# Moving the weight buffers of a fused decoder layer by 896 bytes, and reordering queues around its second batch

## The reference

```
h = rmsnorm(x) * norm_w
q, k, v = heads(h Wq), heads(h Wk), heads(h Wv)      # 8 heads of 64, q and k rotated (rope)
f, g, o = sigmoid(h Wbeta + b), sigmoid(h Wig + b), sigmoid(h Wog + b)
M_t = f_t * M_(t-1) + g_t/8 * k_t v_t^T ;  y_t = (q_t M_t) * o_t      # for each head
x = layernorm(x + y Wout + bout)
r_t = 0.9 r_(t-1) + ctx_t^2 ;  x = layernorm(x + x * r)
# 4096 tokens in 4 micro batches; 8 experts, each 128 tokens of every micro batch
x = layernorm(x + gelu(norm(x) W1_e + b1_e) W2_e + b2_e)      # 512 -> 2048 -> 512
```

## Time and profile before

| | |
|---|---|
| median of 3 runs | 1263.2 us (1260.92 to 1263.53) |
| the profiled execution | 1261.89 us |
| its span, first to last instruction | 1260.1 us |
| TensorE busy | 1240.9 us, 98% of the span |
| VectorE, GpSimd, ScalarE busy | 62%, 59%, 37% |
| DMA | 142 GB/s in the mean |
| granted TensorE clock | 1.00 throughout |

### The profile page before, as it was taken

One profiled execution on the slowest core, in us unless ns is written; L12 is line 12 of the kernel. 1 busy time (PEld: TensorE's weight loads), 2 busy tenths in 40 slices (PEclk: granted clock), 3 DMA queues, 4 the chain that ended last, 5 costly groups with the idle time before them and its releaser, 6 DMA issues.

```text
span 1260.1 us, 19325 instructions
## 1 busy us (share of the span) xinstructions
PE 1240.9 (98%) x6682; PEld 1010.0 (80%) x6682; DVE 782.8 (62%) x1297; ACT 460.9 (37%) x629; POOL 737.7 (59%) x519
## 2 busy tenths in 40 slices
PE   8999999999999999999999999999999999999998
PEld 7777888888888888778888888888888888888886
DVE  5898888888888888953544544634734535445424
ACT  5223333333333322544434443534435344343420
POOL 4876665656566665667457275284385384472651
PEclk9999999999999999999999999999999999999999
DMA  7778887877876786536316235245073073162310
GB/s 274 157 152 161 162 160 154 159 160 160 161 160 155 160 156 123 144 141 242 100 60 225 91 108 197 71 169 180 28 248 126 0 275 100 51 232 94 118 51 33
DMA packets 178107, 179.52 MB, mean 142 GB/s; under 512 B 44732, under 2 KB 121484, under 8 KB 178060
## 3 DMA queue, kind: packets, MB, share of 16 engines
q1 hardware_dynamic: 177548, 178.64, 53.0%
q10 hardware_dynamic: 512, 0.26, 0.1%
HBM read 137.55 MB, written 17.18 MB: 123 GB/s over the span
## 4 chain that ended last, share of the span: by engine, by line
PE 60%; DVE 1%; issue 0%; POOL 0%; ACT 0%; POOLq 0%; DVEq 0%; ACTq 0%
PE qk_ps L87 5%; PE qk_ps L89 5%; PE qk_ps L88 5%; PE v_ps L87 5%; PE v_ps L89 5%; PE v_ps L88 5%; PE gate_ps L87 5%; PE gate_ps L89 5%; PE gate_ps L88 5%; PE s_ps L87 3%; PE s_ps L89 3%; PE s_ps L88 3%; PE y_ps L87 3%; PE y_ps L89 2%; PE y_ps L88 2%
## 5 line engine op out<-in xcount | busy, mean ns | idle before, releaser
L1006 POOL TENSOR_TENSOR w_lo<-w_raw,w_hi 128x2048 fp32r<-128x2048 f32 x31 | 143.4, 4626 | 101.3 <-ACT w_hi L760 101.3
L1342 DVE CAST hid_hi<-gate_ps 128x512 fp32r<-128x512 f32 x62 | 42.8, 690 | 196.8 <-ACT gate_ps L800 184.5
L998 POOL TENSOR_TENSOR w_lo<-w_raw,w_hi 128x2048 fp32r<-128x2048 f32 x32 | 148.0, 4626 | 13.6 <-ACT w_hi L770 13.6
L1088 DVE TENSOR_TENSOR_SCAN decays<-f_all,diag 128x384 f32<-128x384 f32 x128 | 151.0, 1218 | 0.6
L87 PE MATMUL qk_ps<-xT_parts,wqkv_hi 128*128 128x256 f32 x512 | 148.3, 290 | 1.7 <-ACT c_both L688 0.8
L89 PE MATMUL qk_ps<-xT_parts,wqkv_lo 128*128 128x256 f32 x512 | 144.4, 282 | 0.0
L88 PE MATMUL qk_ps<-xT_parts,wqkv_hi 128*128 128x256 f32 x512 | 144.2, 282 | 0.0
L1342 DVE CAST hid_hi<-v_ps 128x512 fp32r<-128x512 f32 x62 | 42.8, 690 | 148.2 <-ACT v_ps L800 148.2
L800 ACT ACTIVATE v_ps<-v_ps,b_cols 128x512 f32<-128x512 f32 x64 | 42.4, 662 | 198.9 <-PE v_ps L89 198.9
L87 PEld LDWEIGHTS qk_ps<-xT_parts,wqkv_hi 128*128 128x128 f32 x512 | 96.4, 188 | 12.7 <-issue 7.9
L800 ACT ACTIVATE gate_ps<-gate_ps,b_cols 128x512 f32<-128x512 f32 x64 | 42.2, 659 | 175.9 <-PE gate_ps L89 175.6
(11 more groups left out here) (238 smaller groups left out, 3221.0 us busy)
## 6 DMA issues: line engine op xcount, KB each, us to landing
w_raw<-in_w SPq DMA_DIRECT2D x64, 1024.0 KB, 7.8
f_all<-f_dram SPq DMA_DIRECT2D x16, 1024.0 KB, 5.0
qkT<-rot SPq DMA_DIRECT2D x256, 64.0 KB, 2.0
xT_raw<-in_xT SPq DMA_DIRECT2D x16, 512.0 KB, 12.9
x_both<-in_x SPq DMA_DIRECT2D x16, 512.0 KB, 11.6
f_all<-f_dram SPq DMA_DIRECT2D x16, 512.0 KB, 6.1
c_both<-in_ctx_in SPq DMA_DIRECT2D x16, 512.0 KB, 13.5
x_both<-x_dram SPq DMA_DIRECT2D x8, 1024.0 KB, 5.0
```

The lines of the kernel that those rows point to most:

```text
L998: pool.tensor_tensor(w2_lo[s % 2][:], w2_raw[s % 2][:], w2_hi[s % 2][:].bitcast(F32), ALU.subtract)\
L1006: pool.tensor_tensor(w1_lo[s % 2][:], w1_raw[s % 2][:], w1_hi[s % 2][:].bitcast(F32), ALU.subtract)\
L1088: dve.tensor_tensor_scan(decays[:, n, :], f_all[:, n, :], diag[:], 0.0, ALU.mult, ALU.add).then_inc(decay_done, 1)
L1342: dve.tensor_copy(high, up_ps[c % 2][:]).then_inc(hid_hi_done, 1)
```

## The change

SBUF_FROM goes up by 896 bytes and wg_parts, which takes 896 bytes, moves from between wqkv_lo and wout_hi to behind res. So wqkv_hi and wqkv_lo (and all that the experts keep in them) move up by 896 bytes, wout_hi to res stay where they were, and the small buffers behind move up by 896.

In the first batches the orders change. TensorE: shares 6 and 7 of batch 1 come ahead of the first scores of batch 0, and share 8 and turn_gates(1) ahead of the second. VectorE: sum_gates(2) ahead of scans 6 and 7 of batch 1; in the last batch scan 6 behind token_low 1 and 2. ScalarE: the gates of batch 2 no longer wait until the scans of batch 1 are done (they had protected f_all); SP waits for that instead, ahead of the loads of f_all. SP: x of batch 3 is loaded behind the moves of batch 1, and the three constants of the experts behind the gates' loads. GpSimd: context_low(0) ahead of the third rotation of batch 1, residual(1) behind the fourth.

```diff
--- before.py
+++ after.py
@@ -45,7 +45,7 @@
 DW = P + L
 RMS_EPS, LN_EPS = 1e-6, 1e-5
 DECAY, THETA = 0.9, 10000.0
-SBUF_FROM = 16512
+SBUF_FROM = 17408
 
 
 class Step:
@@ -127,8 +127,6 @@
 
     wqkv_hi = sb("wqkv_hi", [P, KC, 3 * D], F32R)
     wqkv_lo = sb("wqkv_lo", [P, KC, 3 * D], F32R)
-    wg_parts = sb("wg_parts", [P, KC, LOW_ROW + NG], F32R)
-    wg_hi, wg_lo = wg_parts[:, :, 0:NG], wg_parts[:, :, LOW_ROW:]
     wout_hi = sb("wout_hi", [P, KC, D], F32R)
     wout_lo = sb("wout_lo", [P, KC, D], F32R)
     bout_all = sb("bout_all", [P, 1, D])
@@ -169,6 +167,8 @@
     ctx_parts = sb("ctx_parts", [P, 2 * NT, D], F32R)
     ctx_hi, ctx_lo = ctx_parts[:, 0:NT, :], ctx_parts[:, NT:2 * NT, :]
     res = sb("res", [P, NT, D])
+    wg_parts = sb("wg_parts", [P, KC, LOW_ROW + NG], F32R)
+    wg_hi, wg_lo = wg_parts[:, :, 0:NG], wg_parts[:, :, LOW_ROW:]
     wg_raw = sb("wg_raw", [P, KC, NG])
     normw = sb("normw", [P, KC])
     gate_bias = sb("gate_bias", [NG, 1])
@@ -404,8 +404,8 @@
             def spread_f(b):
 
                 sp.wait_ge(f_stored, b.after(16, 16))
-                if b.n == 1:
-                    sp.wait_ge(decay_done, NH)
+                if b.n in (1, 2) and b.i is None:
+                    sp.wait_ge(decay_done, NH * b.n)
                 rows = f_dram[b.odd, 0:NH * L].rearrange("(h t) -> h t", t=L)
                 sp.dma_start(f_all[:, :, P:DW], rows.partition_broadcast(P)).then_inc(f_in, 16)
                 sp.dma_start(f_all[:, :, 0:P], rows[:, P:L].partition_broadcast(P)).then_inc(f_in, 16)
@@ -481,14 +481,14 @@
                     move(b, 0)
                     spread_rms(b + 1)
                     load_xT(b + 2)
-                    load_x(b + 2)
                     move(b, 2)
                     move(b, 1)
                     move(b, 3)
+                    load_x(b + 2)
+                    following(b + 1)
                     sp.dma_start(gamma_sb[:], gamma).then_inc(e_const_in, 16)
                     sp.dma_start(beta_sb[:], beta).then_inc(e_const_in, 16)
                     sp.dma_start(b1_cols[:], b1).then_inc(e_const_in, 16)
-                    following(b + 1)
                     return
                 if (b + 1).within(B):
                     store_rms(b + 1)
@@ -657,7 +657,7 @@
                 act.wait_ge(gates_summed, b.after(1, 1))
                 if b.n >= 1:
                     act.wait_ge(f_stored, (b - 1).after(16, 16))
-                    if b.n >= 2:
+                    if b.n >= 3 or b.i is not None:
                         act.wait_ge(decay_done, (b - 1).after(NH, NH))
                     if b.n <= 2:
                         act.wait_ge(gates_turned, (b - 1).after(1, 1))
@@ -947,14 +947,14 @@
                     rotate(b, 1)
                 if b.n == 1:
                     x_low(b + 1)
-                    residual(b)
+                    context_low(b - 1)
                 if b.n == B - 1:
                     expert_scale(Step(0), 0)
                 if b.within(B):
                     rotate(b, 2)
-                    if b.n == 1:
-                        context_low(b - 1)
                     rotate(b, 3)
+                if b.n == 1:
+                    residual(b)
                 if b.n == 0:
                     pool.wait_ge(decay_done, 2)
                     residual(b)
@@ -1223,8 +1223,9 @@
                 y_low(b - 1, 3)
                 scans(b, 3)
                 rope_parts(b, 3)
-                scans(b, 4, 5, 6, 7)
+                scans(b, 4, 5)
                 sum_gates(b + 1)
+                scans(b, 6, 7)
                 add_residual(b - 1, 0)
                 add_residual(b - 1, 1)
                 norm_stats(b - 1, 0)
@@ -1260,10 +1261,10 @@
                     scans(b, 5)
                     add_residual(b - 1, 0)
                     token_low(Step(0), 0)
-                    scans(b, 6)
                     token_low(Step(0), 1)
                     add_residual(b - 1, 1)
                     token_low(Step(0), 2)
+                    scans(b, 6)
                 else:
                     sum_gates(b + 1)
                     gate_v(b, 1)
@@ -1519,7 +1520,10 @@
 
             def slot(b, n):
 
-                if b.within(B):
+                if b.n == 1 and n == 2:
+                    project_share(b, 3 * n + 2)
+                    turn_gates(b)
+                elif b.within(B):
                     project_share(b, 3 * n)
                     project_share(b, 3 * n + 1)
                 first = b.n == 1 and n == 0
@@ -1530,11 +1534,11 @@
                         up(Step(0), k // KC, k % KC)
                 if (b - 1).within(B) and n in (2, 4, 6):
                     weighted_values(b - 1, n // 2 - 1)
-                if b.within(B):
+                if b.within(B) and not (b.n == 1 and n == 2):
                     project_share(b, 3 * n + 2)
-                    if n == 2 and b.n == 1:
-                        turn_gates(b)
                 if b.n == 1 and n == 1:
+                    project_share(b, 3 * n + 3)
+                    project_share(b, 3 * n + 4)
                     scores(b - 1, 0)
                 if (b - 1).within(B) and n == NH - 1:
                     weighted_values(b - 1, n // 2)
```

## The result

The changed kernel takes **1252.92 us** in the median of 6 runs (1250.22 to 1253.69), the kernel before 1262.45 on the same chip (6 runs, 1260.69 to 1263.53): ratio 0.9924, 95% interval 0.9911 to 0.9937, 9.5 us less. The forecast was 13 us. The profiled execution took 1253.3 us, span 1251.5 against 1260.1.

What follows compares the result with a forecast made beforehand. TensorE, busy 1240.9 of 1260.1 us, was taken as the bound, with VectorE sharing the batch loop. Terms -10.6 - 1.7 - 0.7 = -13.0 us gave 1248.9 profiled, median 1249.5; range 1244 to 1257.

Steps and rivals of the forecast that it cites:

- Placement in the experts: Expert matmuls: operands agreeing within 256 bytes cut the mean step from 230.3 to 226.85 ns, -10.6 us (-9.2 to -12.0).
- Rival A: Experts: operand place is not the cause of the slow steps, so only small gains remain, 1261.5 us; chance 12%.
- variant about low memory: Experts: something special about the low part of memory makes steps slow, so 896 bytes do not matter; within the 12%.
- rival B: Experts: matched pairs of wqkv with an outside buffer become the slower ones, +9.7 us, about 1271; chance 3%.
- Loop: Batch stage: 48 q/k matmuls of 256 columns in each of 12 batches gain 3 ns, -1.7 us (0 to -3.6).
- q/k steps under 118: Sign of being right, batch stage: steps of 256-column q/k matmuls fall below 118 ns, from 118.5.
- First scores: Batch 0: shares ahead of the scores fill a 1.48 us wait, but scores still wait for DMA: 0, ends +0.5 and -0.5.
- GpSimd and SP, waits at 66.96 and 71.36: Early batches: the 0.71 us wait for ctx_parts goes, and most of the 1.15 us wait for qkT.
- What of this arrives: Start of batch 3: it hangs on SP's store_rms(3), so only -0.7 us of 2.7 us of waits (0 to -2.7; +1).
- The bound of +1: Start of batch 3, unfavourable end: +1 us if SP's issues behind the x load wait for it instead.
- Last batch: The 0.70 us wait before its scores mostly goes, but moved scan 6 delays the second scores: 0, ends -0.7 and +0.5.
- Rival C: Batches 1 to 3: late x of batch 3 delays ScalarE beyond VectorE's 2.67 us cover, +5.3 us, 1255; chance 7%.

Runs made afterwards that it cites:

- placement alone: The kernel before with only the buffers moved, all orders as before: 1250.67 us, ratio 0.9900; repeated on another occasion 1250.71 us, ratio 0.9908.
- orders alone: The changed kernel with the old buffer placement, so only the orders differ from the kernel before: 1265.01 us, ratio 1.0017.
- 17280: The changed kernel with the wqkv buffers 128 bytes lower, at address 17280, buffers from wout_hi on kept: 1264.77 us in one run.
- 17152: The changed kernel with the wqkv buffers 256 bytes lower, at address 17152, buffers from wout_hi on kept: 1251.74 us in one run.
- best version: The kernel before with the buffers moved and the gamma, beta and b1 loads moved to the batch before the last: 1247.60 us, ratio 0.9888.

## Why the prediction was right and wrong

**Direction, main cause and range held; the size was 3.5 us too hopeful**, mostly by the orders, which cost instead of giving, and by a loss in the last batches. The experts gave a little more than forecast and so hid part of it.

*Placement in the experts* (-10.6): right. The step fell from 230.3 to 226.7 (174.08/768), 3.67 ns x 3072 = -11.3; the last stretch shrank by 11.45. It is more than forecast because the 227.3 of some matched groups, which I took as one of two ends, came from their neighbours. In the kernel before, the group at 896.98 has a first step of 231 ns and then 226 to 227. Matched groups that follow a mixed one take longer to settle, 230 to 231 ns in the mean: the one at 907.96 begins 236, 224, 231, 236, 228, 232, 231, and only then 227. I had not looked at those. Now the neighbours match as well. Rival A is excluded by placement alone and orders alone, and its variant about low memory by 17280 and 17152; rival B by the absence of groups that became slower.

The rule of the Trainium skill that I set against the rows ("SBUF — State Buffer", section "Who interferes with whom": PE never waits on anyone) did not decide here. With nothing changed but an address, the same matmul takes 226.7 or some 233 ns. What in the machine does that, no run tells.

*Loop* (-1.7): wrong, in the step "I take 3" ns for 256 columns, with bounds of 0 to 6.3. The price has the other sign. TensorE's timeline in the changed kernel, a run of q/k shares as in the earlier trace rows:

```profile
240.53 0.28 PE L88 MATMUL qk_ps<-xT_parts,wqkv_hi 128*128 128x256 f32 x1
...
244.60 0.28 PE L89 MATMUL qk_ps<-xT_parts,wqkv_lo 128*128 128x256 f32 x1
```

(244.60 - 240.53)/34 = 119.7 ns, and 120 in single steps once settled, where the mixed pairs took 118.5. A matched pair of 256 columns is 1.2 ns slower, not 3 faster: 48 x 12 x 1.2 = +0.7 us. Scaling the 512-column price down was the mistake; a shape without a row of its own should have had bounds on both sides of zero. The loop in all took 0.8 us less in this trace, but between 356.7 and 357.8 in nine traces with the new placement, against 357.6 in the one trace before, so the placement's effect on it can't be told. What differs is again, it seems, which scan meets GpSimd: a batch in which the second scan behind cross_memory takes 2.1 us lasts 32.6 to 32.8 us, the others 32.3 to 32.4. Of the eleven batches five were such before and two after, which makes about the 0.8. The signs to look for said "q/k steps under 118": they missed.

*First scores* (0): right, as worked out. Scores at 38.48 for 38.55, and v waits for gate_v up to 46.34, close to the 45.67 + 0.69 named.

*GpSimd and SP, waits at 66.96 and 71.36* (gone, without worth): right. The new waits are the one for VectorE's probs (2.9 us) and the 1.4 at 108.00 in place of 0.81. I had said about 2, ending near 105.

*What of this arrives* (-0.7, "+1 if the issues behind the x load wait for it instead"): wrong, and this is the larger miss. It came out at +2.4 in this trace; the orders cost 1.4 us in one timed pair and 2.2 in the other. The step "SP's queue holds the same issues in another order" counted issues at their old price. The twelve moves gave the 0.7 us back (8.72 to 8.04). But load_g and spread_o took 2.2 us more. In six traces with x ahead of the moves the two take 7.5 to 8.0 us, in eight with x right ahead of f_all 8.2 to 10.7. Their issues last while f_all travels: in nine of the fourteen traces the second g_raw issue ended within 0.2 us of the landing of the first f_all load. That x holds f_all up is an inference from these times. And "f_all of batch 2 leaves without the three constant loads ahead of it" was true and left out its other half: they now stand between the end of that block and store_rms(3), and take 1.6 us there (84.61 to 86.22), about the 1.9 that they had taken ahead of f_all (72.86 to 74.75). From the first of these issues to store_rms(3) it was 20.8 us (from 63.56), and is now 22.4 (from 63.81). The bound of +1 had the right mechanism and too small a size. I put it as an end and not as a rival, and so gave it no weight in the number.

*Last batch* (0, ends -0.7 and +0.5): the 0.70 us wait went and scan 6 did nothing that can be told. The +1.1 comes from a meeting of engines that I hadn't looked for.

*Rival C* (ScalarE late through x): its mechanism shows, far smaller than its price. ScalarE waits 4.65 us for x, and VectorE behind it 0.41 us at 80.08. VectorE's cover held.

Sum by the measured terms: -11.45 - 0.8 + 2.4 + 1.1 + 0.1 = -8.6 us of span.

## What to carry to other kernels

Where an engine is 98% busy, look at the distance between single starts, grouped by which buffers the operands lie in. Equal instructions at two paces may be time to be had without touching the schedule; here some 11 us for moving buffers by 896 bytes. Look at every shape by itself: what helped 512 columns slightly hurt 256. When a queue is reordered, price each issue at what it blocks for in its new place, and ask what each moved piece now stands in front of: here three small loads took 1.9 us of the queue in one place of the chain and 1.6 in the other, and none only outside of it. Then try the parts one by one, since the good part may be carrying the others: the placement with the old orders, and the constants out of the way, takes 1247.6 us, 4.5 less than the whole change on the same chip.

## What the runs showed of the hardware

- In the experts, a 512-column fp32r matmul takes 226.7 ns from start to start when its two operands' addresses agree within 256 bytes and its neighbours' do too, and mostly 232 to 234 when they differ by 64 or by 128; agreement within 512 or 1024 isn't needed (17152). It takes several matmuls to settle after a change. The twelve v products of a batch, which stand between attention matmuls, show little of it: 231.1 ns in agreement, 231.7 at a difference of 128.
- With 256 columns it is 119.5 to 119.8 in agreement, 118.4 to 118.8 at a difference of 128, and 117.8 or 113.3 at 64.
- The time that a DMA issue takes on SP depends on its place: the two g_raw issues took 5 to 6.6 us where x had been issued right ahead of f_all, and 3.5 to 5.3 where x had gone ahead of the moves. In the best version the second ended at 77.01, and the first f_all load landed at 77.02.
- A scan of 0.95 us takes 1.9 us beside a GpSimd rotation. Whether the rotation starts 0.19 us ahead of the scan or 0.15 behind its start decides. In the last batches the first 1.0 us of it costs nothing, and what goes beyond goes into the time one for one.
- Around the end of TensorE's wait of 2.9 us its granted clock was 0.70 in a stretch of 5 us and 0.96 in the next, at no cost, as TensorE had to wait again. Behind waits of 2.2 to 2.4 us right ahead of a run of q and k products it was 0.66 to 0.77 in one stretch, and the way to cross_memory(2) took 1.3 to 1.5 us longer.
